# Two 8-expert mixtures of a six-stage kernel: token rows go to fixed regions of each expert by running rank, group by group; weights are loaded once; biases of the second layer are added after the tiles

## The reference

```python
def _L1_ffn_ref(x, Wg, bg, W1, b1, W2, b2):
    DIM, FF, E = (128, 512, 8)
    probs = jax.nn.softmax(x @ Wg + bg, axis=-1)
    h = jax.nn.relu(jnp.einsum('bsd,edf->bsef', x, W1) + b1)
    all_out = jnp.einsum('bsef,efd->bsed', h, W2) + b2
    top_vals, top_idx = jax.lax.top_k(probs, 2)
    weights = top_vals / (jnp.sum(top_vals, axis=-1, keepdims=True) + 1e-09)
    selected = jnp.take_along_axis(all_out, top_idx[..., None], axis=2)
    return jnp.sum(selected * weights[..., None], axis=2)
...
x = x + 0.5 * _L0_ffn_ref(_layernorm(x, axis=-1), ...)
x = x + _L0_attn_ref(_layernorm(x, axis=-1), ...)
x = x + 0.5 * _L0_ffn_ref(_layernorm(x, axis=-1), ...)
x = x + 0.5 * _L1_ffn_ref(_layernorm(x, axis=-1), ...)
x = x + _L1_attn_ref(_layernorm(x, axis=-1), ...)
x = x + 0.5 * _L1_ffn_ref(_layernorm(x, axis=-1), ...)
```

## Time and profile before

| | us |
|---|---|
| runs | 1254.29, 1250.93, 1252.24 |
| median | 1252.24 |
| profiled execution, own time | 1252.09 |
| its span | 1250.3 |
| stage f0 | 179.8 |
| stage a0 | 202.8 |
| stage g0 | 185.8 |
| stage f1 | 170.0 |
| stage a1 | 339.7 |
| stage g1 | 166.6 |

### The profile page before, as it was taken

One profiled execution on the slowest core, in us unless ns is written; L12 is line 12 of the kernel. 1 busy time (PEld: TensorE's weight loads), 2 busy tenths in 40 slices (PEclk: granted clock), 3 DMA queues, 4 the chain that ended last, 5 costly groups with the idle time before them and its releaser, 6 DMA issues.

```text
span 1250.3 us, 25112 instructions
## 1 busy us (share of the span) xinstructions
PE 982.0 (79%) x7978; PEld 738.3 (59%) x7978; DVE 812.6 (65%) x2665; ACT 573.8 (46%) x1503; POOL 296.7 (24%) x333
## 2 busy tenths in 40 slices
PE   4599866999996599895369918999999999624992
PEld 3245765667764245684249906666667666423992
DVE  4875787578775876787445554767777667561554
ACT  3202563356564201463125514777787778501551
POOL 1201117232201200200745523000000000055552
PEclk9699896699997699896579967999999999857997
DMA  8004016000006002208540116554335541554113
GB/s 229 1 0 114 1 48 168 1 1 2 2 1 177 20 0 61 54 1 176 165 115 29 32 69 185 153 169 119 120 118 153 169 119 52 89 169 119 31 34 105
DMA packets 131422, 105.39 MB, mean 84 GB/s; under 512 B 7988, under 2 KB 118108, under 8 KB 131317
## 3 DMA queue, kind: packets, MB, share of 16 engines
q1 hardware_dynamic: 126772, 95.55, 27.9%
q0 software_dynamic: 4544, 8.54, 2.1%
HBM read 66.14 MB, written 38.83 MB: 84 GB/s over the span
## 4 chain that ended last, share of the span: by engine, by line
PE 56%; DVE 21%; issue 11%; SPq 5%; ACT 3%; DMA 2%; POOL 2%; DVEq 0%; PEld 0%; POOLq 0%; ACTq 0%; PEldq 0%
PE psum L561 6%; PE psum L944 6%; PE psum L570 5%; PE psum L1029 5%; PE psum L1554 3%; PE psum L1603 3%; PE psum L322 2%; PE psum L2024 2%; PE psum L2069 2%; PE psum L2036 2%; DVE a_L L2194 2%; PE psum L1016 2%; SPq L454 1%; PE psum L324 1%; PE psum L323 1%
## 5 line engine op out<-in xcount | busy, mean ns | idle before, releaser
L1734 DVE TENSOR_REDUCE a_negmax<-psum 128x2 f32<-128x512 f32 x128 | 84.3, 685 | 37.1 <-PE psum L1554 36.4
L1171 DVE TENSOR_TENSOR g_S<-g_place,g_number 128x512 bf16<-128x512 f32 (+1 forms) x116 | 76.7, 701 | 17.6 <-PEq L939 6.0
L1683 ACT ACTIVATE a_PT<-psum 128x1024 f32<-128x1024 f32 x64 | 65.5, 1024 | 28.5 <-PE psum L1586 28.2
L601 ACT ACTIVATE g_hT<-psum,g_tile_bias 128x128 f32<-128x128 f32 x156 | 44.6, 368 | 73.1 <-PE psum L561 73.0
L1171 DVE TENSOR_TENSOR f_S<-f_place,f_number 128x512 bf16<-128x512 f32 (+1 forms) x100 | 66.2, 704 | 16.0 <-PEq L939 6.1
L2140 ACT ACTIVATE a_pr<-a_L,a_least 128x128 f32<-128x128 f32 x128 | 50.5, 395 | 54.3 <-DVE a_least L2194 54.2
L601 ACT ACTIVATE f_hT<-psum,f_tile_bias 128x128 f32<-128x128 f32 x156 | 44.6, 368 | 63.5 <-PE psum L561 63.5
L1554 PE MATMUL psum<-a_turned 24*128 24x256 f32 x256 | 59.6, 355 | 6.6 <-DVE a_negmax L1734 6.4
L2142 ACT ACTIVATE a_pr<-a_L,a_least 128x256 f32<-128x256 f32 x128 | 63.3, 495 | 0.0
L2024 PE MATMUL psum<-a_KT,a_Q 64*128 64x128 f32 (+1 forms) x512 | 59.6, 351 | 1.4 <-DVE a_least L2194 1.4
L2150 ACT ACTIVATE a_PT<-psum 128x384 f32<-128x384 f32 x128 | 55.6, 488 | 1.9 <-PE psum L2036 1.7
(11 more groups left out here) (528 smaller groups left out, 2879.8 us busy)
## 6 DMA issues: line engine op xcount, KB each, us to landing
z<-a_G SPq DMA_DIRECT2D x32, 512.0 KB, 3.3
a_X<-z SPq DMA_DIRECT2D x16, 1024.0 KB, 6.8
a_X<-z SPq DMA_DIRECT2D x16, 512.0 KB, 3.9
f_wgu<-in_gate_up SPq DMA_DIRECT2D x16, 384.0 KB, 6.6
z<-pad SPq DMA_DIRECT2D x6, 1024.0 KB, 9.8
g_wgu<-in_gate_up SPq DMA_DIRECT2D x16, 384.0 KB, 6.9
f_w<-in_W SPq DMA_DIRECT2D x16, 256.0 KB
g_w<-in_W SPq DMA_DIRECT2D x16, 256.0 KB
```

Of the source, the lines that this page charges most:

```text
L601: act.activation(hT[:, i % 2, c, :], bank[i % 2][:, P * c:P * c + P], ACT.Relu, bias=tile_bias[:, c, i:i + 1]).then_inc(relu_done, 1)
L1171: return dve.tensor_tensor(S[:, slot, :].rearrange("p (t e n) -> p t e n", t=1, n=CAPACITY), bcast(place[:, ds(t, 1), CE * k:CE * k + CE], ...
L1683: act.activation(PT[m % 4][:, :, :, :].rearrange("p j t n -> p j (t n)"), core.psum[:, 2 + 2 * (u % 2):4 + 2 * (u % 2), :], ACT.Exp, scale ...
L1734: dve.tensor_reduce(negmax[:, :, h], bank[h % 2].rearrange("p (t n) -> p t n", n=SEQ), AX.X, ALU.max, negate=True).then_inc(max_done, 1)
```

## The change

The head becomes a class `Front` that works on four groups of four tiles. Every expert owns a fixed region of 2048 rows of `slots_dram` (135 tiles in all), so that a slot number is the region's start plus the token's rank so far, and needs no count of all tokens. VectorE normalises three groups, routes group 0, normalises group 3, then writes the slots of group 0, and so on; GpSimd scatters 8 transfers a group as soon as that group's slots are there. Which 39 of the 135 tiles hold tokens is worked out by VectorE meanwhile (`tile_at`); SyncE loads their numbers into registers, the first 14 before the scatters end, and loads each tile by its own transfer, 39 in place of four.

`Experts` loads the weights once, in f1, with b1 in four transposed transfers; the biases of the tiles now come from one group of four matmuls and a copy of ScalarE. `Fills` fills the regions of both mixtures in a0, by two transfers from GpSimd's `empty`, each 17280 rows of 528 bytes. The weighting's 13 operations (`weigh`) stand one by one behind `y_out` in the passes 6 to 18. The transposes of `ex` and the matmuls with `b2` stand behind the last pass. TensorE's wait ahead of the unused matmuls is now for the even groups 0 and 2, and WARM is 14. Of the last additions VectorE keeps the first two quarters as they were; ScalarE scales the rows of the other two, VectorE adds one of these with two operations of 128x512 and GpSimd the other. YBUF is 5. In a1, X0, X1, Q and KT have one buffer in place of two.

```diff
+class Front:
...
+    K, ROW, REGION = 2, 132, TOKENS
...
+    def scatter(self, pool, g):
+        for k in range(self.K):
+            for t in range(self.group):
+                at = self.slot[:, k, self.group * g + t:self.group * g + t + 1]
+                pool.indirect_dma_start(self.slots_dram[:, :], bass.IndirectOffsetOnAxis(ap=at, axis=0),
+                                        self.rows[:, g % self.ring, k, t, :], None,
+                                        bounds_check=E1 * self.REGION, oob_is_err=False).then_inc(
+                                            self.rows_sent[g % 2][0], 16)
...
+    def rank(self, pe, g, out):
+        G, core = self.group, self.core
+        flat = self.sel[:, self.tiles(g), :].rearrange("p t e -> p (t e)")
+        each = lambda ap: ap.unsqueeze(1).to_broadcast([ap.shape[0], G, E1])
+        pe.wait_ge(self.sel_ready, g + 1)
+        pe.matmul(out[:, 0:G * E1], core.tri[:, :], flat, start=True, stop=False, skip_group_check=True)
+        for d in range(1, G):
+            pe.matmul(out[:, E1 * d:G * E1], core.ones[:, :], flat[:, 0:E1 * (G - d)], start=False, stop=False,
+                      skip_group_check=True)
+        if g:
+            pe.wait_ge(self.run_ready, g)
+            pe.matmul(out[:, 0:G * E1], core.ones[:, :], each(self.run[:, g, :]), start=False, stop=False,
+                      skip_group_check=True)
+        pe.wait_ge(self.offset_filled, 1)
+        return pe.matmul(out[:, 0:G * E1], core.ones[0:1, :], each(self.offset[:, :]), start=False, stop=True,
+                         skip_group_check=True)
...
+    def route(self, dve, step, g, ps, read=None):
+        K, G, tiles = self.K, self.group, self.tiles(g)
+        if not g:
+            dve.wait_ge(self.absent_filled, 1)
+            dve.wait_ge(self.loaded, 32)
+        step(dve.tensor_tensor(self.logit[:, tiles, 0:E1], ps[:, 0:G * E1].rearrange("p (t e) -> p t e", e=E1),
+                               self.bg[:, :].unsqueeze(1).to_broadcast([P, G, E1]), ALU.add))
...
+        for t in range(G):
+            last = dve.max(self.top[:, t, :], self.logit[:, G * g + t, :])
+        step(last)
...
+        for t in range(G):
+            last = dve.match_replace(self.repl[:, t, :], self.top[:, t, :], self.logit[:, G * g + t, :], self.TAKEN)
+        step(last)
+        step(dve.tensor_scalar(self.sel[:, tiles, :], self.repl[:, :, 0:E1], 1.0e38, None, ALU.is_gt))
+        dve.sem_inc(self.sel_ready, 1)
...
+    def places(self, dve, step, g, ps, read=None):
+        G, tiles = self.group, self.tiles(g)
+        step(dve.tensor_tensor(self.place[:, tiles, :], ps[:, 0:G * E1].rearrange("p (t e) -> p t e", e=E1),
...
+            dve.sem_inc(read, 1)
+        dve.tensor_reduce(self.both[:, tiles], self.place[:, tiles, :], AX.X, ALU.add)
+        step(dve.tensor_reduce(self.where[:, 1, tiles], self.place[:, tiles, :], AX.X, ALU.max))
+        step(dve.tensor_tensor(self.where[:, 0, tiles], self.both[:, tiles], self.where[:, 1, tiles], ALU.subtract))
```

```diff
+class Fills:
...
+    def sync(self, sp):
+        sp.wait_ge(self.empty_filled, 2)
+        source = self.empty[:, :, :].rearrange("p a n -> p (a n)").unsqueeze(1)
+        for slots in self.slots:
+            sp.dma_start(slots[1:1 + P * self.PER, :].rearrange("(p r a) n -> p r (a n)", p=P, a=self.ROWS),
+                         source.to_broadcast([P, self.PER // self.ROWS, self.ROWS * Front.ROW])).then_inc(self.emptied, 16)
+        sp.wait_ge(self.emptied, 16 * len(self.slots))
...
-    YBUF = 6
...
+    YBUF = 5
...
-    GROUPS = ((0, 2), (2, 8), (8, 22), (22, PASSES))
...
-    WARM = 18
...
+    GROUPS = ((0, 1), (1, 2), (2, 4), (4, 8), (8, 14), (14, 22), (22, PASSES))
...
+    EARLY, WARM = (14, 14) if alone else (3, 24)
```

```diff
-        wait_sent(sp, rows_sent, 16 * (K * TILES - LAST))
-        wait_sent(sp, last_sent, 16 * LAST)
+        regions = fr.slots_dram[1:1 + Front.TILES_OUT * SLOTS, :].rearrange("(a p) n -> p a n", p=P)
+        sp.wait_ge(at_ready, 1)
+        def number(i):
+            return sp.value_load(tile_at[0:1, i:i + 1], min_val=0, max_val=Front.TILES_OUT - 1)
+        first_numbers = [number(i) for i in range(EARLY)]
+        wait_sent(sp, even_sent, fr.rows_total(0))
+        wait_sent(sp, odd_sent, fr.rows_total(1))
         for g, (first, end) in enumerate(GROUPS):
-            sp.dma_start(xin[:, first:end, :], slots_dram[SLOTS * first:SLOTS * end, :]
-                         .rearrange("(a p) n -> p a n", p=P)).then_inc(x_loaded[g], 16)
+            for i in range(first, end):
+                at = first_numbers[i] if i < EARLY else number(i)
+                sp.dma_start(xin[:, i:i + 1, :], regions[:, ds(at, 1), :]).then_inc(x_loaded[g], 16)
...
+        pool.wait_ge(b2_added, 4)
+        for k in range(K):
+            pool.wait_ge(back_scaled, 4 * (K + k + 1))
+            xq = core.x[:, 12:16, :]
+            pool.tensor_tensor(xq, xq, back[:, 12:16, k, :], ALU.add).then_inc(last_added, 1)
+            pool.wait_ge(last_added, k + 1)
```

```diff
+        pe.wait_ge(fr.run_ready, fr.groups)
+        pe.matmul(ps_count, core.ones[:, :], fr.run[:, fr.groups, :], start=True, stop=True).then_inc(counted, 1)
...
+        core.experts.wait(pe)
+        pe.wait_ge(owned, 1)
+        for c in range(FC1):
+            last = pe.matmul(bank[1][:, PASSES * c:PASSES * c + PASSES], b1[:, c, :], tile_own[:, :], start=True, stop=True)
+        last.then_inc(bias_done, 1)
...
+        wait_sent(pe, even_sent, fr.rows_total(0))
+        some = fr.sel[:, :, :].rearrange("p t e -> p (t e)").unsqueeze(1).to_broadcast([P, 4, P])
         for i in range(WARM):
-            pe.matmul(bank[4], core.ones[:, :], sel_flat, start=True, stop=True)
```

```diff
+        pe.wait_ge(weights_ready, 1)
+        pe.wait_ge(xT_ready, PASSES)
+        for t in range(TILES):
+            last = pe.transpose(bank[B2_BANKS[t // 4]][0:E1, P * (t % 4):P * (t % 4) + P], ex[:, t, :], core.ident[:, :])
+            if t % 4 == 3:
+                last.then_inc(ex_turned, 1)
+        for q in range(4):
+            pe.wait_ge(exT_ready, q + 1)
+            for t in range(4 * q, 4 * q + 4):
+                last = pe.matmul(bank[B2_BANKS[q]][:, P * (t % 4):P * (t % 4) + P], exT[:, P * t:P * t + P], b2[:, :],
+                                 start=True, stop=True)
+            last.then_inc(b2_done, 1)
     def scalar(act):
...
+        act.wait_ge(weight_ready, 1)
+        for q in (2, 3):
+            act.wait_ge(back_loaded[q], 16)
+            for k in range(K):
+                for t in range(4 * q, 4 * q + 4):
+                    act.activation(back[:, t, k, :], back[:, t, k, :], ACT.Copy,
+                                   scale=weight[:, k, t:t + 1]).then_inc(back_scaled, 1)
...
+            fr.statistics(dve, step)
+            def route(g):
+                dve.wait_ge(fr.logits_done, g + 1)
+                fr.route(dve, step, g, bank[4 + g])
+            def places(g):
+                fr.count(dve, step, g)
+                dve.wait_ge(fr.ranked, g + 1)
+                fr.places(dve, step, g, bank[4 + g])
+            for g in range(3):
+                fr.normalise(dve, g)
+            route(0)
+            fr.normalise(dve, 3)
+            places(0)
+            for g in range(1, fr.groups):
+                route(g)
```

```diff
+        step(dve.tensor_reduce(tile_skip[:, :], tile_pick[:, :, :], AX.X, ALU.add))
+        step(dve.tensor_tensor(tile_at[:, :], tile_skip[0:1, :], tile_number[0:1, :], ALU.add))
+        dve.sem_inc(at_ready, 1)
...
-        step(dve.tensor_reduce(total[:, :], ex[:, :, :], AX.X, ALU.add))
-        step(dve.tensor_tensor(ex[:, :, :], ex[:, :, :], taken[:, :, :], ALU.mult))
-        step(dve.tensor_reduce(den[:, :], ex[:, :, :], AX.X, ALU.add))
...
+        def weigh(part_no):
+            if part_no == 0:
+                dve.wait_ge(exp_done, 1)
+                step(dve.tensor_reduce(total[:, :], ex[:, :, :], AX.X, ALU.add))
+            elif part_no == 1:
+                step(dve.tensor_tensor(ex[:, :, :], ex[:, :, :], fr.sel[:, :, :], ALU.mult))
...
                 y_out(i - 1)
+            if i >= 6:
+                weigh(i - 6)
         y_out(PASSES - 1)
+        for q in range(4):
+            dve.wait_ge(b2_done, q + 1)
+            xq = core.x[:, 4 * q:4 * q + 4, :]
+            dve.tensor_tensor(xq, xq, bank[B2_BANKS[q]].rearrange("p (t d) -> p t d", d=P), ALU.add).then_inc(b2_added, 1)
...
-        for q in range(4):
+        for q in range(2):
...
+        for k in range(K):
+            dve.wait_ge(back_scaled, 4 * (k + 1))
+            xq = core.x[:, 8:12, :]
+            step(dve.tensor_tensor(xq, xq, back[:, 8:12, k, :], ALU.add))
...
-                    sp.wait_ge(l_ready, H1 * (b - 2) + RH * (c + 1))
+                if b:
+                    sp.wait_ge(l_ready, H1 * (b - 1) + RH * (c + 1))
...
-                    sp.dma_start((X0, X1)[q][s][:, heads, :], turned).then_inc(x_turned[s][c], 16)
```

(1 more changed line is left out.)

497 lines of the change are left out of this document (311 added, 186 removed).

## The result

The changed kernel measured slower: 1261.36 us (median of 20 runs, 1246.3 to 1265.0) against 1251.08 for the kernel before (20 runs, 1238.1 to 1262.5), a ratio of 1.0067 with a 95% interval of 1.0045 to 1.0088. The prediction was 1238, faster, with a range up to 1259. On two other chips the same kernel stood at 1.0026 (0.9984 to 1.0068) and 1.0014 (0.9978 to 1.0050) against the kernel before. These ratios leave out executions over 1.5% above the fastest of their kernel, four of the twelve of the third comparison among them; by the medians of all executions the changed kernel is 10.3, 4.8 and 7.4 us above the kernel before. All three say that the 14 us of gain did not come.

What follows compares the result with a forecast made beforehand. Each mixture's path was taken as head, 32 scatters, 39 passes, return, additions. Terms -20.3 + 4.4 + 3.2 - 1.4 = -14.1 took 1252.1 to 1238 us; forecast 1231 to 1246, range 1231 to 1259.

Steps and rivals of the forecast that it cites:

- Head: Start of f1 and g1: scatters start after 4 token tiles instead of 16, 11.6 and 8.7 us earlier; sum -20.3.
- Weighting: Passes 6 to 18: 13 small operations between VectorE's copies, at half their serial price, 2.2 us a mixture; +4.4.
- rival 2: Costs take their upper bounds: weighting 8.8, clock 6.2, end 0, head -18; 1249 us, no measurable change; chance 0.15.
- Clock at the first pass: TensorE pauses before the first tile, so passes run some 3 us at half pace: +1.6 a mixture, +3.2.
- Tile loads, fills, weights, single buffers: SyncE's single tile loads, fills in a0, weights loaded once, a1's single buffers: all off the path, 0 each.
- The end: Behind the last pass: second biases hidden by the rows' return, last additions shared; 8.7 against 9.36 us, -1.4 in all.
- Rival 1: Second biases' 8-row matmuls release late, now behind the passes: +17.6 a mixture, 1275 us, slower; chance 0.16.
- Rival 3: In the head, each group's places are released late, first scatter no earlier, added costs stay: 1258 us; chance 0.06.
- The lock on the shared ports: Last quarters: if VectorE and GpSimd exclude each other, one GpSimd addition waits some 0.65 us, sum 1.3 higher.

Runs made afterwards that it cites:

- weigh_ahead: Changed kernel with the 13 weighting operations moved from passes 6 to 18 to ahead of VectorE's first copy of weights; 1252.1 us, 0.9998 of the kernel before.
- warm_44: Changed kernel with 44 unused matmuls instead of 14 ahead of the first tile; 1253.5 us, 1.0005 of the kernel before.

## Why the prediction was wrong

Step by step, in the order of its sum (f1 and g1 together):

- **Head, -20.3: right.** First scatter at 16.6 and 16.4 us into the stages, -18.5. The slots came 0.9 us later than worked out, since the first group's logits wait for eight transposes at the low clock (578.35 to 580.4). The later groups kept GpSimd busy, as said.
- **Weighting, +4.4: right.** +4.2 (from the sixth y to the 19th), confirmed by `weigh_ahead`. That half of the serial price would come of it was a guess, and it came out; rival 2, with the whole price, did not happen.
- **Clock at the first pass, +3.2: right in kind, a little small.** +4.2 in the trace, 4.4 and 2.7 in the two others, 4.8 between the changed kernel and `warm_44`. The granted clock stayed at 1.2 GHz for 6.1 and 5.1 us of the passes, not for 3.
- **Tile loads, fills, weights, single buffers, all 0: right.** Behind the first two tiles TensorE never waited for a load, and the fills went at 362 GB/s in a0, 51 us instead of the 120 worked out from one fill's pace. Passes 19 to 39 took 1.0 us more in f1, which was not foreseen; 0.4 of it is gone in `weigh_ahead`, and the other 0.6 is the alternation told of there.
- **The end, -1.4: this step failed.** It asked for the last addition and found it 0.2 us earlier in f1, but 1.8 later in g1, where the last rows of y took longer to land: the chain has 3.74 us for them against 2.14 in f1, and no run shows why. Above all it took the last addition for the end of the stage. The stage ends when every engine has drained, and GpSimd's drain, 5.9 us behind 71 indirect transfers, was moved onto the path by the two additions: +5.8 in each mixture, +11.6. The term stood in the trace before: the row of L2262 has 7.15 us for it in the kernel before. The prediction had gone through what GpSimd's additions wait for, and not through what waits for GpSimd.
- **Rival 1 (the 8-row matmuls end late behind the passes, 1275): wrong.** They took 3.83 us and every quarter was released in time. The doubt that kept its chance at 0.16, that the late releases stood beside scatters, was the right one. The Trainium skill, TensorE: Matmul & The Clock Gate, section "Why this matters for your kernels", gives a matmul over few rows (its case is 32) the time of one over 128. This trace agrees: 32 over 8 rows in 3.83 us, 0.12 each, beside 0.13 for those over 128 rows (8 in 1.06). What made the releases of the kernel before late lies beside the scatters and is not settled.
- **Rival 3 (the places are released late, 1258): wrong.** The first scatter came 10.7 and 7.8 us earlier; its chain of matmuls was released in time.
- **The lock on the shared ports.** At the end of the mixtures it was not put to the test: VectorE's additions of the third quarter ended at 733.0, GpSimd's two began at 733.27 and took 2.60 together, and they do not meet in any of the seven traces that have them. But the 1.71 us of the earlier trace rows, which the prediction takes as a hint, can be looked up in f0 of the kernel before:

```profile
134.01 1.23 DVE L1171 TENSOR_TENSOR f_S<-f_place,f_number 128x512 bf16<-128x512 bf16 x1 [0.47 <-PEq L1008]
134.65 1.71 POOL L313 TENSOR_TENSOR f_ypart<-f_ys,f_ypart 128x512 fp32r<-128x512 f32 x1
135.16 1.75 DVE L1171 TENSOR_TENSOR f_S<-f_place,f_number 128x512 bf16<-128x512 bf16 x1
```

  Both engines' operations have two inputs in on-chip memory. VectorE's two of this line that meet GpSimd's additions are stretched, and so is the addition that began while one of them ran; the other 98 of VectorE's 100 took 0.68 to 0.69 us, the other seven of GpSimd's eight 1.26 to 1.27. In g0 it is the same (1.75 and 1.71). The Trainium skill, SBUF — State Buffer, section "SBUF: two separate sides", has the two engines share one pair of ports under an exclusive lock, and these rows agree with it.
- **The range.** Sum of the terms that were wrong: drain +11.6, return +3.0, head +1.8, clock +1.0, late passes +0.8, weighting -0.2, together 18 of the 24 us between -14.1 and +9.9. The other 6.3 are f0, a0, g0 and a1, and they are chance as far as the traces tell: f0 took 167.2 to 168.0 us in ten of the 20 traces and 172.1 to 172.7 in the other ten, the code of both kernels among each, and a0, g0 and a1 vary as shown above. The range allowed for none of that, though it is larger than most terms: the kernel before alone spread from 1238 to 1262 over 20 executions. Without this part the profiled execution would have come to some 1256, inside the range but on the wrong side of the kernel before; the drain alone turns the gain of the forecast into next to none.

## What to carry to other kernels

Work that is moved to the last place of a stage moves the engine's own ending with it. Before giving an engine the last step, look up its drain and whatever else it issues behind that step; if it must be last, drain it while it waits. And cover with something cheap any pause of TensorE that the change opens just ahead of a dense stretch; 30 more unused matmuls were worth 4.8 us here.

When single executions spread by more than the effect, read the effect at fixed places of the trace from the start of the stage. Two traces made the fills look guilty here; 18 more and the medians did not bear it out.

## What the runs showed of the hardware

- GpSimd's drain takes 5.9 us behind 71 indirect transfers and two additions, 6.8 to 7.5 us right behind the last transfer, 1.5 to 2.2 us in stages without indirect transfers, and 0.04 us if another drain stands ahead of the last two additions. It is not down to nothing when the transfers have long landed: in f1 of the changed kernel the last had landed at 151.7 us of the stage, and the drain that began at 164.8 took 5.87.
- Beside a row of indirect scatters VectorE, SyncE and probably TensorE can fall to one instruction per 0.7 us (three of the six groups, in f1 and g1 alike, from 5 to 7 us after the first scatter to 4 or 5 us after the last). Why it happens on some chips only is open.
- In stretches whose VectorE operations are the same to 0.2 us, the granted clock went up for good at 58 us in one execution and at 85 in another: 10.8 us of 203 in a0 (of which g0 mostly gave 4 back). In a1 it went up at 42 or at 55 us: 4.0 us of 339.
- GpSimd's and VectorE's operations with two inputs in on-chip memory stretch each other where they overlap: 1.71 us in place of 1.27, and 1.23 and 1.75 in place of 0.69 (f0 of the kernel before).
